# Last stage of a fused attention kernel: two turned operands by transposing transfers, VectorE's turn written in another order, and a mask product issued earlier

## The reference, cut to what matters

```python
h = einsum('bhid,oi,od->bho', x, weighted_sum, weight)   # 512 positions; the text's 77 are appended
h = h + attn(layernorm(h))       # attention over the batch of 8, 16 heads of 16, q and k normalised
h = h + ffn(layernorm(h))

def ffn(x):                      # the last stage
    n = rmsnorm(x, gamma1)
    q = n @ Wq + bq;  k, v = split((n @ Wdown + bdown) @ Wup + bup)
    att = softmax(q_heads @ k_heads.T / 4)       # 16 heads against 16 heads of the same token
    x2 = x + (att @ v) @ Wo + bo
    h2 = rmsnorm(x2, gamma2)
    gate = softmax(h2 @ Wg + bg)                 # 8 experts
    return x2 + sum_e gate[e] * (h2 @ We[e])
```

## Time and profile before

| | |
|---|---|
| median of 3 runs | 799.55 us |
| profiled execution | 801.38 us |
| its span, first to last instruction | 799.3 us |
| PE busy | 745.6 us (93%) |
| DVE busy | 703.5 us (88%) |
| POOL busy | 409.4 us (51%) |
| ACT busy | 374.4 us (47%) |
| mean granted TensorE clock | 0.981 |

### The profile page before, as it was taken

The page is one execution under the profiler, slowest core; times in us unless marked ns, Lnnn a source line. Parts: engine busy times, 40 slices in busy tenths (PEclk is TensorE's granted clock), DMA queues, the critical chain, the costliest instruction groups (busy, mean ns, idle before and its releaser), DMA issues.

```text
span 799.3 us, 48197 instructions
## 1 busy us (share of the span) xinstructions
PE 745.6 (93%) x20274; PEld 508.0 (64%) x20274; DVE 703.5 (88%) x1591; ACT 374.4 (47%) x985; POOL 409.4 (51%) x1094
## 2 busy tenths in 40 slices
PE   4999978999999999876999999999999999999997
PEld 3888855666666666654656666666666666666553
DVE  5798778999999999765799999999999999999987
ACT  4478544665566665543333443344344434343321
POOL 1231355555666667444455665566556655665411
PEclk9999999999999999987899999999999999999999
DMA  9987000000000000000011001100111011101100
GB/s 331 326 252 228 3 3 4 2 0 0 0 0 0 0 0 2 11 17 10 15 26 28 23 16 26 26 23 16 26 26 26 14 26 26 26 13 27 29 16 20
DMA packets 38377, 33.25 MB, mean 42 GB/s; under 512 B 24786, under 2 KB 33570, under 8 KB 38314
## 3 DMA queue, kind: packets, MB, share of 16 engines
q1 hardware_dynamic: 38314, 32.35, 13.4%
HBM read 22.64 MB, written 4.83 MB: 34 GB/s over the span
## 4 chain that ended last, share of the span: by engine, by line
PE 39%; DVE 10%; issue 3%; DVEq 0%
PE bank L204 9%; PE bank L205 8%; PE bank L206 8%; PE bank L957 5%; PE bank L946 5%; DVE acc L1099 3%; DVE smax L1108 2%; PE bank L964 1%; DVE res L1099 1%; PE bank L977 1%; PE bank L1016 1%; PE bank L1003 1%; PE bank L1002 1%; DVE fq_t L1147 1%; DVE logits L1117 1%
## 5 line engine op out<-in xcount | busy, mean ns | idle before, releaser
L1099 DVE SCALAR_TENSOR_TENSOR acc<-bank,gate,acc 128x256 f32<-128x256 f32 x222 | 106.1, 478 | 12.8 <-PE bank L206 4.1
L204 PE MATMUL bank<-we_h,h_t_h 128*128 128x512 f16 x296 | 113.0, 382 | 3.7 <-DVE res L1099 1.0
L205 PE MATMUL bank<-we_l,h_t_h 128*128 128x512 f16 x296 | 112.2, 379 | 0.6 <-issue 0.6
L206 PE MATMUL bank<-we_h,h_t_l 128*128 128x512 f16 x296 | 112.2, 379 | 0.0
L204 PE MATMUL bank<-tokw_h,x_t_h 128*128 128x256 f16 x256 | 71.0, 277 | 11.3 <-DVE x_t_l L682 11.3
L1053 ACT ACTIVATE junk<-x 128x256 f32<-128x256 f32 x37 | 15.4, 417 | 120.4 <-DVE x L1143 120.4
L205 PE MATMUL bank<-tokw_l,x_t_h 128*128 128x256 f16 x256 | 70.9, 277 | 0.0
L206 PE MATMUL bank<-tokw_h,x_t_l 128*128 128x256 f16 x256 | 70.8, 277 | 0.0
L1188 POOL TENSOR_TENSOR t<-ss,rms_ws 128x1 f32<-128x1 f32 x37 | 7.1, 192 | 117.1 <-ACT junk L1053 117.1
L287 PE MATMUL bank<-vaug,pr_t 32*32 32x17 f32 x4736 | 49.8, 181 | 10.7 <-issue 10.7
L957 PEld LDWEIGHTS bank<-pr_t,v 32*32 32x32 f32 x4736 | 47.6, 104 | 18.7 <-issue 18.3
(11 more groups left out here) (223 smaller groups left out, 2232.8 us busy)
## 6 DMA issues: line engine op xcount, KB each, us to landing
xbuf<-in_x SPq DMA_DIRECT2D x32, 512.0 KB, 5.3
out<-res SPq DMA_DIRECT2D x36, 128.0 KB
we_s<-in_we SPq DMA_DIRECT2D x4, 512.0 KB, 7.3
inw<-in_in_w SPq DMA_DIRECT2D x1, 768.0 KB, 11.6
hn_t_h<-hn_r_h SPq DMA_TRANSPOSE x37, 2.3
hn_t_l<-hn_r_l SPq DMA_TRANSPOSE x37, 2.4
wrep<-in_w_rep SPq DMA_DIRECT2D x1, 512.0 KB, 4.8
h_all<-in_txt SPq DMA_DIRECT2D x1, 512.0 KB
```

What stands on the lines that cost most here:

```text
L204: nc.tensor.matmul(dst, a_h(c), b_h(c), start=start and c == 0, stop=False)
L205: nc.tensor.matmul(dst, a_h(c), b_l(c), start=False, stop=False)
L206: last = nc.tensor.matmul(dst, a_l(c), b_h(c), start=False, stop=stop and c == chunks - 1)
L1099: op = nc.vector.scalar_tensor_tensor(out=(res if e == E - 1 else acc)[:, :], in0=b_we[s % 2][:, k * D:(k + 1) * D], scalar=gate[p][:, e:e ...
```

## The change

- Last stage, `fon` and `x2`: TensorE's four transposes of a turn go. ScalarE copies the high part to rows (`on_r[0]`, `x2_r[0]`), GpSimd makes the low part of `fon` (`on_r[1]`), VectorE that of `x2` (`x2_r[1]`), and SP turns each by a transposing transfer. SP's turn is now fon high, fon low, hn high, hn low, out, x2 high, x2 low.
- TensorE: the projection of q stands ahead of the gate's product, and the product with Wo behind the sums.
- VectorE: `combine` takes one expert at a time, and the calls are spread among the other operations; x2 now stands behind the reciprocal of the sums.
- Queries are turned without a stride; tokens are paired otherwise, so that `fq_t[q, :, pair]` and `kv_t[q, :, pair]` have one stride. The mask constant follows.
- The gate's product is one `scalar_tensor_tensor` with the reciprocal as a broadcast tensor, in place of a `tensor_scalar` with two column scalars.
- GpSimd: the low part of `hn` is made one turn later relative to its tile and earlier in the turn, with the coefficients behind it.
- Attention stage: the mask product waits only for its bank and its constants; the scores wait for `a_qkt`. VectorE takes the reciprocal ahead of the addition to `h_all`.

```diff
 # attention stage, TensorE
-                    pe.wait_ge(a_qkt, i + 1)
                     wait(pe, a_sub, i)
+                    pe.wait_ge(a_qkm, i + 1)
                     nc.tensor.matmul(b_s[:, :], am[:, 0:P], am[:, P:], start=True, stop=True,
+                    if not first:
+                        settle(pe, c_in)
+                        pe.wait_ge(a_qkt, i + 1)
                     scores(range(0, 4))
 # last stage, TensorE
-                if real(i, -1):
-                    pe.wait_ge(f_on, i)
-                    wait(pe, f_h2l, i - 1)
...
-                        last = nc.tensor.transpose(b_turn[:, c * P:(c + 1) * P],
...
                 if real(i, 1):
                     pe.wait_ge(hn_in, 32 * (i + 2))
...
+                if real(i, -2):
+                    pe.wait_ge(x2_in, 32 * (i - 1))
+                    wait(pe, f_x2, i - 1)
+                    rows_times(b_gate, *h2_t[p], lambda c: wg_h[:, c, :], lambda c: wg_l[:, c, :]).then_inc(f_gate, 1)
                 experts(i, p, 0)
...
+                if real(i, -1):
+                    pe.wait_ge(on_in, 32 * i)
+                    wait(pe, f_logit, i - 1)
+
+                    rows_times(b_wo, fon_h, fon_l, lambda c: wo_h[:, c, :], lambda c: wo_l[:, c, :]).then_inc(f_wo, 1)
                 experts(i, p, 2)
-                if real(i, -1):
-                    pe.wait_ge(f_x2, i)
-                    for c in range(KC):
-                        last = nc.tensor.transpose(b_turn[:, c * P:(c + 1) * P], x2[:, c * P:(c + 1) * P], ident[:, :])
-                    last.then_inc(f_h2ps, 1)
 # last stage, ScalarE
                 if real(i, -1):
                     act.wait_ge(f_x2, i)
+                    wait(act, x2_in, 32 * (i - 1))
+                    nc.scalar.activation(x2_r[0][:, :], x2[:, :], ACT.Copy).then_inc(f_x2h, 1)
 # last stage, VectorE
-                    nc.vector.tensor_scalar(gate[p][:, :], gexp[:, :], grec[:, :], r2[p][:, :], ALU.mult,
-                                            ALU.mult).then_inc(f_gmul, 1)
+                    nc.vector.scalar_tensor_tensor(out=gate[p][:, :], in0=gexp[:, :], scalar=r2[p][:, :],
+                                                   in1=grec[:, :].to_broadcast([P, E]), op0=ALU.mult,
+                                                   op1=ALU.mult).then_inc(f_gmul, 1)
...
+                combine(i, p, 4)
+                if real(i, -1):
+                    dve.wait_ge(f_x2h, i)
+                    wait(dve, x2_in, 32 * (i - 1))
+                    nc.vector.tensor_tensor(x2_r[1][:, :], x2[:, :], x2_r[0][:, :], ALU.subtract).then_inc(f_x2l, 1)
+                combine(i, p, 5)
 # SP
+                        sp.dma_start_transpose(fon_h[:, :, :], on_r[0][:, :]).then_inc(on_in, 16)
+                        sp.wait_ge(p_onl, i)
+                        sp.dma_start_transpose(fon_l[:, :, :], on_r[1][:, :]).then_inc(on_in, 16)
...
+                        sp.wait_ge(f_x2h, i)
...
+                        sp.dma_start_transpose(x2_t[0][:, :, :], x2_r[0][:, :]).then_inc(x2_in, 16)
+                        sp.wait_ge(f_x2l, i)
+                        sp.dma_start_transpose(x2_t[1][:, :, :], x2_r[1][:, :]).then_inc(x2_in, 16)
```

More of the change, by code:

```diff
@@ L1082, in ffn_dve, with combine @@
         def ffn_dve(dve):
-            def combine(i, p, s):
+            def combine(i, p, e):
                 if not real(i, -2):
                     return
[L1087 to L1090, removed]
-                else:
[L1092 to L1102, removed]
+                s, k = divmod(e, EP)
+                if k:
+                    dve.wait_ge(f_acc, (i - 2) * STEPS + s + 1)
+                else:
+                    dve.wait_ge(f_we, (i - 2) * STEPS + s + 1)
+                    if s:
+                        dve.wait_ge(f_comb, (i - 2) * STEPS + s)
+                    else:
+                        dve.wait_ge(f_gmul, i - 1)
+                        dve.wait_ge(p_hx2, i - 1)
+                if e == E - 1:
+                    wait(dve, out_done, (i - 2) * 16)
+                nc.vector.scalar_tensor_tensor(
+                    out=(res if e == E - 1 else acc)[:, :], in0=b_we[s % 2][:, k * D:(k + 1) * D],
+                    scalar=gate[p][:, e:e + 1], in1=(acc if e else hx2[p])[:, :], op0=ALU.mult,
+                    op1=ALU.add).then_inc(f_comb if k else f_acc, 1)
@@ L1141, in body @@
                     wait(dve, f_ss2, i - 1)
-                    wait(dve, f_h2ps, i - 1)
+                    wait(dve, f_x2l, i - 1)
                     nc.vector.scalar_tensor_tensor(out=x2[:, :], in0=b_wo, scalar=1.0 / WS, in1=x1b[:, :],
                                                    op0=ALU.mult, op1=ALU.add).then_inc(f_x2, 1)
[L1145 to L1161, removed]
-                    nc.vector.reciprocal(frsum[:, :], of[:, :, HD:HD + 1]).then_inc(f_rsum, 1)
@@ L1177, in body, with coefs @@
+            def coefs(i):
+                if real(i, AHEAD) and real(i, 0):
+                    ffn_coefficients(pool, i + AHEAD)
+            def body(i, p):
+                filling = isinstance(i, int) and i <= 0
+                if real(i, -1):
+                    pool.wait_ge(f_onh, i)
+                    nc.gpsimd.tensor_tensor(on_r[1][:, :], fon[:, :, :].rearrange("p h d -> p (h d)"), on_r[0][:, :],
+                                            ALU.subtract).then_inc(p_onl, 1)
                 if real(i, 1):
@@ L1185, in body @@
                     nc.gpsimd.tensor_tensor(lat_l[0:LAT, :], lat[:, :], lat_h[0:LAT, :], ALU.subtract).then_inc(p_latl, 1)
+                if real(i, 2) and not filling and not (isinstance(i, int) and i == 1):
+                    low(i + 2)
+                if not filling:
+                    coefs(i)
                 if real(i, -1):
```

133 lines of the change are left out of this document (73 added, 60 removed).

## The result

The changed kernel takes 868.88 us, the median of four runs (866.45 to 873.57), against 800.19 (798.84 to 803.93) before: 1.084 times as long, 95% interval 1.079 to 1.088. That is +69 us where the forecast had +36, and outside its range of 786 to 857. The profiled execution took 866.45 us, its span 864.3, so 65.0 more than the span before.

What follows compares the result with a forecast made beforehand. VectorE's list bounded the 11.45 us turn, TensorE just behind; afterwards x2's loop would, at 12.6 us. 801.4 - 5 (attention) + 38 (33 turns) + 4 (ends) = 838, median 836 us; range 786 to 857.

Steps and rivals of the forecast that it cites:

- The gate's product in the form of the logits is 216 in place of 375 ns: VectorE's list, last stage: the gate's product in its new form saves 0.16 us a turn.
- the 7.7 us from the logits to x2: VectorE's stretch in a last-stage turn: 8.6 us less 0.3 queries, 0.16 gate and 0.44 interleaved pairs.
- attention stage: Reordered VectorE work saves 0.2 us a turn; -5 us over 25 full turns, not above 0 or below -8.
- The stride moves from writing the queries to reading `kv_t`: VectorE, last stage: `v` takes 0.34 us more if the strided read costs what the strided write did.
- the interleaving: VectorE, last stage: separating dependent operations saves 0.10 to 0.12 us a pair; four pairs, 0.44 us, between logits and x2.
- The scores with a stride: TensorE, last stage: strided operands add between nothing and half of 1.24 us; taken as nothing, PE having time to spare.
- the loop and its trip: Last stage: x2's copy, transfers, landing and gate matmuls take 4.97 us to the logits; the loop closes at 12.6 us.
- SP's and GpSimd's lists at nothing: Last stage: six transfers a turn on SP and one more 0.7 us GpSimd operation add no time.
- the rise of the last turns: End of the last stage: x2 to logits goes from 2.54 to 4.97 us in two turns, +4 us for both.
- The trip is hidden: Rival, last stage: TensorE's work covers x2's transfer, turns of 11.0 to 11.25 us, 780 to 788 us; chance 0.13.
- The trip is longer: Rival, last stage: landings of 3.4 us and `v` 0.34 dearer, 13.8 us a turn, 877 us; chance 0.08.
- The clock falls: Rival, last stage: a less busy PE gets a lower granted clock, time passes 900 us; chance 0.03.

Runs made afterwards that it cites:

- experiment 12: Changed kernel with GpSimd's low part of `hn` ahead of the latents' low part (`lat_l`): 854.26 us, 1.066 of the kernel before.
- experiment 1: Changed kernel with the gate's product as `tensor_scalar` again: 869.9 us, 1.085 of the kernel before.
- 5: Changed kernel with GpSimd's `hn_r_l` moved behind the coefficients: 870.26 us, 1.086 of the kernel before.
- experiment 7: Changed kernel with VectorE's subtraction of the scores ahead of the logits: 860.54 us, 1.072 of the kernel before.
- experiment 3: Changed kernel with the old arrangement of queries, keys and values (queries written with a stride): 863.24 us, 1.074 of the kernel before.
- 9: Changed kernel with x2 and Wo's product made earlier, plus the old arrangement of queries and keys: 798.0 us, 0.997 of the kernel before.
- experiment 10: Kernel of 9 with GpSimd's `hn_r_l` ahead of `lat_l`: 789.44 us, 0.986 of the kernel before.
- 11: Kernel of experiment 10 with VectorE's subtraction of the scores ahead of the logits: 790.43 us, 0.988 of the kernel before.
- experiment 6: Changed kernel with Wo's product ahead of experts' step 2 and x2 behind the third combining operation, transfers unchanged: 813.09 us, 1.014 of the kernel before.

## Why the prediction was wrong

- **The step that failed** is "The gate's product in the form of the logits is 216 in place of 375 ns", which went into the 7.7 us from the logits to x2. The product took 0.83 us. Free it does take 0.23; what the step leaves out is that it waits out the GpSimd operations beside it, and the change moved `hn_r_l` right behind `lat_l`, onto the product. This is 0.6 us a steady turn. Of the 28 us by which the profiled time exceeded the forecast for it (838 to 866.45) it makes 20, counted by 33 steady turns, or 16, by the whole stretch in experiment 12. Experiments 1, 5, 7 and 12 show the mechanism, 12 the price. The old price was a mean over held and free turns, and the alternation between them (0.29 and 0.46 us) stood in the trace of the kernel before.
- **The rest of the 28 us**: attention stage 2, the tail 1, the steady turn without the hold 12.67 instead of 12.6 (2), and single turns longer than the steady ones 3 (the mean is 13.36, the steady turn 13.27). The longest of them stands beside a clock of 0.80; which part of it the clock makes stays open.
- **"The stride moves from writing the queries to reading `kv_t`; if that read costs what the strided write did, `v` takes 0.34 more"**: it did, 0.32. The sum left it at nothing without a reason. By itself that is 0.32 x 33, some 11 us, and it didn't show only because other terms of the same stretch erred the other way. From start to start, one turn before against one of experiment 12, the interleaving saved 0.60 us in this stretch and not 0.44, and the gate's product, which the turn taken as the base had held at 0.46, gave back 0.23 and not 0.16. So that experiment 12 comes to 7.75 us where 7.7 was forecast is in part luck.
- **The scores with a stride** were taken at nothing, with a bound of half more (0.62 us); they took 0.74 us more, beyond the bound. "PE will turn out to have over a microsecond to spare right behind them" held in the changed kernel (experiment 3) and not once the loop was opened (9).
- **Right**: the loop and its trip (4.94 against 4.97 us, landing 2.4, issue 1.22), the place and kind of the waits, `fq_t` at 701 ns, the rise of the last turns (4.9 against 4), SP's and GpSimd's lists at nothing apart from the hold. Right in sign but too large: the attention stage, 2.9 us against 5. Its steady turns gained more than was said, 6.10 us on average against 6.37, but they began 1.5 us later (156.59 against 155.14). The last of them begins 5.0 us earlier (309.32 against 314.32), and where the stages meet 2.1 of these are lost.
- **The rivals.** *The trip is hidden* was wrong for this change, but its condition was right. Once x2 stood early the loop opened, and 9 to 11 came near its 780 to 788 us, with 789 to 798. The rule of the Trainium skill named there (DMA: Bandwidth & Descriptors, "Rules for kernel authors": issue early, wait late) agrees with experiment 6: there are the same six transfers, x2's issued earlier, and no steady turn waits for them. *The trip is longer* had nearly the right size (13.8 us a turn) partly by luck: of its two causes the strided read of `v` was there (0.32) and the longer landings, the larger one, were not (2.4 at the median). *The clock falls* came only as short dips, and the mean granted clock went from 0.981 to 0.966.

## What to carry to other kernels

Before pricing a small operation, look at it one by one in the timeline, not at its mean: one that ends together with a GpSimd operation again and again has been waiting for it, and in a new place it may wait for a longer one. A trip of 4.9 us cost its whole length here while producer and consumer stood at the two ends of the same list, and nothing once the value was made half a turn ahead. A stride that is moved from one operand to another is not removed.

## What the runs showed of the hardware

- **VectorE and GpSimd exclude each other for some operations.** The gate's product, its tensors all in SBUF, takes 0.23 us free (0.29 in the `tensor_scalar` form) and lasted 0.46 (before), 0.83 or 1.06 us beside GpSimd, until GpSimd's run ended. Both forms were held alike (experiment 1). The other way round, GpSimd's small `t` takes 0.19 us in the changed kernel. In experiment 10 it starts 0.02 behind VectorE's `x_r_l`, takes 0.44 and ends with it:

```profile
488.39 0.41 DVE L1147 TENSOR_TENSOR x_r_l<-x,x_r_h 128x256 f16<-128x256 f32 x1
```

```profile
488.41 0.44 POOL L1202 TENSOR_TENSOR t<-ss,rms_ws 128x1 f32<-128x1 f32 x1
```

Operations that read a bank were not held: x2 took 0.41 to 0.42 us beside GpSimd's work and without it (experiments 9 and 10). The Trainium skill (SBUF — State Buffer, "SBUF: two separate sides") calls it an exclusive lock that whoever starts first holds for its whole instruction; experiment 7 agrees (0.11 us ahead: free; 0.01 behind: held). That the hold ran on from `lat_l` into `hn_r_l` behind it isn't explained by this; before, it ended in most held turns with `qpad`, although `lat_l` followed as closely.
- **The next operation in the same position is `fon`**: 414 ns in the changed kernel, 832 to 836 in experiments 9 and 10, where it starts beside GpSimd's `x1b` (0.73 us). So the fastest kernel may have some 0.4 us a turn left, an estimate from these two numbers; moving `x1b` wasn't tried.
- **A 32x32-blocked transposition of 128x512 float32** takes 0.70 us dense and 1.03 with a 64-byte stride, whether this stands on the write (`fq_t`) or on the read (`v`). The 128 small float32 matmuls with such a stride on both operands take 2.03 us instead of 1.3 to 1.5 (experiments 9 and 3).
